# Selective-scan block with sparse attention: states as four n by 32 channels instead of two n by 64, ring buffers cut to four states and two C slots, ScalarE's copies moved one step behind TensorE, tails moved one step earlier

## The reference, cut to what matters

```python
# layer 1, a selective scan (DIN = 256 channels, N = 16 states)
xc, r = split(x @ W_in); xs = causal_conv4(xc) + conv_b; u = silu(xs)
dbc = u @ W_x                       # 128 columns for delta, 16 for B, 16 for C
delta = softplus(dbc[:128] @ W_dt + b_dt)
h[d,n] = exp(delta[d] * A[d,n]) * h[d,n] + delta[d] * u[d] * B[n]     # over 512 tokens
y[d]   = sum_n h[d,n] * C[n] + u[d] * D[d]
x1 = layernorm(x + (y * silu(r)) @ W_out + xs)
# layer 2, on the 64 tokens of each sequence with the highest router score
sel = top_k(x1 @ w_router, 64); attention over the 256 chosen rows, gated MLP, scatter back
out = layernorm(2 * x1 + change)
```

## Time and profile before

| | |
|---|---|
| three runs | 498.07, 494.09, 494.52 us; median 494.52 |
| profiled execution | 495.5 us, of it 493.8 us span from the first to the last instruction |
| mean granted TensorE clock | 0.948 of full |
| busy in the span | TensorE 415.6 us (84%), VectorE 308.5 (62%), ScalarE 310.8 (63%), GpSimd 285.6 (58%) |
| the loop, first to last scan | 58.5 to 345.2 us |
| chain that ended last | TensorE 42%, ScalarE 18%, VectorE 11%, issue 9%, GpSimd 8% |

### The profile page before, as it was taken

The page is one execution under the profiler, slowest core; times in us unless marked ns, Lnnn a source line. Parts: engine busy times, 40 slices in busy tenths (PEclk is TensorE's granted clock), DMA queues, the critical chain, the costliest instruction groups (busy, mean ns, idle before and its releaser), DMA issues.

```text
span 493.8 us, 6513 instructions
## 1 busy us (share of the span) xinstructions
PE 415.6 (84%) x2021; PEld 251.6 (51%) x2021; DVE 308.5 (62%) x600; ACT 310.8 (63%) x674; POOL 285.6 (58%) x261
## 2 busy tenths in 40 slices
PE   5988898799999799799867789775967888999991
PEld 4433453444445344346324356342754767887881
DVE  0302573587666599882689967999387266554355
ACT  4255688983786994476794486961584597543142
POOL 2010187686987889677889769995472144332012
PEclk9998999979999999899997799989987999999997
DMA  6102501005101004201003215760400000000013
GB/s 231 45 0 84 133 23 43 21 2 156 60 23 42 23 1 98 74 24 40 8 17 72 82 41 168 232 263 0 172 0 3 0 1 1 2 0 1 1 43 128
DMA packets 18710, 29.11 MB, mean 59 GB/s; under 512 B 2698, under 2 KB 10676, under 8 KB 18420
## 3 DMA queue, kind: packets, MB, share of 16 engines
q1 hardware_dynamic: 18676, 28.70, 18.6%
HBM read 22.27 MB, written 2.23 MB: 50 GB/s over the span
## 4 chain that ended last, share of the span: by engine, by line
PE 42%; ACT 18%; DVE 11%; issue 9%; POOL 8%; POOLq 0%; DVEq 0%; ACTq 0%
PE bank L536 7%; PE bank L552 6%; ACT loop_buf L1025 5%; ACT front_a L1035 5%; PE bank L673 4%; POOL state L1561 3%; PE bank L849 3%; PE bank L825 3%; PE bank L617 2%; ACT state L1059 2%; PE bank L639 2%; DVE state L1185 2%; PE bank L857 1%; PE bank L574 1%; ACT state L1060 1%
## 5 line engine op out<-in xcount | busy, mean ns | idle before, releaser
L1185 DVE TENSOR_TENSOR_SCAN state<-front_a,bank 128x512 f32<-128x512 f32 x88 | 102.7, 1205 | 44.6 <-PE bank L536 22.9
L536 PEld LDWEIGHTS bank<-ident,loop_buf 128*128 128x128 f32 x512 | 60.5, 146 | 84.4 <-issue 41.2
L536 PE MATMUL bank<-ident,loop_buf 128*128 128x128 f32 x512 | 85.3, 290 | 18.4 <-ACT loop_buf L1025 17.1
L1035 ACT ACTIVATE front_a<-loop_buf,a_neg 128x512 f32<-128x512 f32 x128 | 84.6, 712 | 8.2 <-DVE copy L1185 5.4
L1025 ACT ACTIVATE loop_buf<-copy,b_rows 128x256 f32<-128x256 f32 x190 | 78.9, 495 | 0.1
L552 PE MATMUL bank<-front_c,conv_raw 128*128 128x512 f32 x128 | 60.8, 608 | 3.3 <-ACT front_c L900 2.0
L1185 DVE TENSOR_TENSOR_SCAN copy<-front_a,bank 128x512 f32<-128x512 f32 x40 | 47.3, 1209 | 24.7 <-PE bank L536 11.5
L1561 POOL TENSOR_TENSOR state<-state,front_a 128x1024 f32<-128x1024 f32 x22 | 53.1, 2417 | 9.5 <-DVE state L1185 9.4
L1561 POOL TENSOR_TENSOR state<-state,c_own 128x1024 f32<-128x1024 f32 x22 | 52.0, 2368 | 9.8 <-DVE state L1185 9.1
L673 PE MATMUL bank<-state,fold 128*64 128x512 f32 x176 | 50.2, 648 | 0.8 <-POOL state L1561 0.8
L1574 POOL TENSOR_TENSOR loop_buf<-copy,b_rows 128x512 f32<-128x512 f32 x31 | 33.6, 1083 | 26.0 <-ACT copy L900 23.2
(11 more groups left out here) (203 smaller groups left out, 759.1 us busy)
## 6 DMA issues: line engine op xcount, KB each, us to landing
front_a<-c_stage SPq DMA_DIRECT2D x32, 128.0 KB, 2.8
c_own<-c_stage SPq DMA_DIRECT2D x32, 128.0 KB, 2.9
loop_buf<-front_b SPq DMA_DIRECT2D x32, 128.0 KB, 2.4
copy<-in_L_attn_x SPq DMA_DIRECT2D x4, 512.0 KB, 3.7
front_b<-in_L_ffn_wo SPq DMA_DIRECT2D x1, 2048.0 KB, 10.0
copy<-in_L_ffn_wq SPq DMA_DIRECT2D x1, 2048.0 KB, 8.2
out<-loop_buf SPq DMA_DIRECT2D x3, 512.0 KB, 3.0
conv_raw<-in_L_attn_conv_w SPq DMA_DIRECT2D x2, 512.0 KB, 3.9
```

The source lines that it names most:

```text
L536: return pe.transpose(dst, src, ident[:])
L1035: act.activation(decay[:, u % NDA, :], delta_wide[:, b % 2, k, :], ACT.Exp, scale=a_neg[:, k, m:m + 1]).then_inc(decay_made, 1)
L1185: dve.tensor_tensor_scan(state[t % NH][:, j, :], decay[:, u % NDA, :], bank[BU_BANK[u % NBU]][:], 0.0, ALU.mult, ALU.add).then_inc(scanned, 1)
```

## The change

The state tile becomes four values of n by 32 channels: a group is four n, four groups per batch, eight units per group. `fold` becomes 128 by 32, and one `add_states(w)` serves two steps with four matmuls into the four partition quarters of the bank, at column positions 0, 32, 64, 96; it runs at odd t. Z of a group has four instructions per chunk; ScalarE does one chunk per step in three of four steps, GpSimd one instruction of 1,024 elements per group at t % 4 == 1, no longer one ahead of its turn at t = 0. `delta_wide` has a slot per 32 channels (eight per batch, ring of 12), widened by 32 DMAs of 32 partitions per batch. `c_wide` has two slots, each filled by four DMAs. The state ring has four buffers. SBUF that this frees and needs is balanced by storing x1 of each batch to DRAM and loading all of it back (2 MB) before the output; ScalarE's `la` waits for the previous batch's gather, choice and store. ScalarE drains in step t what belongs to step t-1, between the two decays. Fronts and tails move by up to three steps; four one-hot instructions become one, two rank additions become one reduction. The reload order of weights changes: w_v, w_o, w_dn are issued together, behind the store of b2's x1 and ahead of the last C slot.

```diff
-    -24: ("xT0", "xT1"), ... -13: ("su", "r0", "r1"), -12: ("dt",), -11: ("bc",),
-    -10: ("rs", "cr", "dl0", "dl1"), -9: ("s1",), -8: ("s2",), -7: ("s3",), -6: ("s4",), -5: ("s5", "s6"),
-    -3: ("du0", "du1"),
+    -25: ("xT0", "xT1"), ... -13: ("su", "r0", "r1"), -12: ("dt", "bc"),
+    -10: ("rs", "cr", "dl0", "dl1", "s1"), -9: ("s2",), -8: ("s3",), -7: ("s4",), -6: ("s5", "s6"),
+    -5: ("du0", "du1"),
...
-    2: ("y0", "y1", "g0", "g1"), 4: ("o0",), 5: ("o1",), 6: ("ls0", "ls1"), 7: ("lp0", "lp1"),
-    8: ("la0", "la1"), 9: ("lx0", "lx1", "ld0", "ld1"), 10: ("sb",), 11: ("k0",), 12: ("k1",), 13: ("k2", "k3"),
-    14: ("pf",), 15: ("ga", "cs"),
+    1: ("y0", "y1", "g0", "g1"), 3: ("o0",), 4: ("o1",), 5: ("ls0", "ls1"), 6: ("lp0", "lp1"),
+    7: ("la0", "la1"), 8: ("lx0", "lx1", "ld0", "ld1"), 9: ("sb", "k0", "k1"), 10: ("k2", "k3"),
+    13: ("pf",), 15: ("ga", "cs"),
...
-        NDA, NBU, NH, NZ, NCW = 4, 4, 6, 2, 4
+        NDA, NBU, NH, NZ, NCW = 4, 4, 4, 2, 2
+        KB, NDW = 4 * KD, 12
...
+            def widen_delta(b, h):
+                sp.wait_ge(delta_ready, KD * b + h + 1)
+                for j in range(4):
+                    slot = KB * b + 4 * h + j
+                    if slot >= NDW:
+                        b0, k0 = (slot - NDW) // KB, (slot - NDW) % KB
+                        sp.wait_ge(decay_made, 2 * NST * b0 + KB * (NQ - 1) + k0 + 1)
+                    for i in range(4):
+                        sp.dma_start(delta_wide[slot % NDW][i * QP:(i + 1) * QP, :],
+                                     delta[j * QP:(j + 1) * QP, h, :]).then_inc(in_delta[4 * h + j], 16)
+            def store_x1(b):
+                sp.wait_ge(rows_ready, 2 * (b + 1))
+                sp.dma_start(x1_stage[b], x1[:, :, 0:DM]).then_inc(x1_stored, 16)
...
+            widen_delta(0, 0)
+            widen_delta(0, 1)
             load_x(2)
+            for g in range(NCW, B * NQ - 2):
+                b, m = g // NQ, g % NQ
                 widen_c(g)
+                if m == 0:
+                    widen_delta(b, 1)
+                elif m == 2 and b >= 1:
+                    store_x1(b - 1)
+                elif m == 3:
+                    if b == 0:
+                        load_x(3)
+                    widen_delta(b + 1, 0)
+            widen_c(B * NQ - 2)
+            store_x1(B - 2)
...
             load("w_v", w_v, wv.rearrange("(k p) n -> p k n", p=P))
-            widen_c(B * NPAIR - 3)
             load("w_o", w_o, wo.rearrange("(h p) n -> p h n", p=P))
-            widen_c(B * NPAIR - 2)
             load("w_dn", w_dn, w_down.rearrange("(f p) n -> p f n", p=P))
-            widen_c(B * NPAIR - 1)
+            widen_c(B * NQ - 1)
...
+            store_x1(B - 1)
+            sp.wait_ge(x1_stored, 16 * B)
+            sp.dma_start(x1_all, x1_stage.rearrange("b p c d -> p b c d")).then_inc(x1_loaded, 16)
...
-                for j in range(2):
-                    mm = pe.matmul(bank[Y_BANK[h]][j * P // 2:(j + 1) * P // 2, :], fold[:], state[t % NH][:, j, :],
-                                   start=(m == 0), stop=(m == NPAIR - 1))
+                pe.wait_ge(weighed, 2 * w + 2)
+                for j in range(4):
+                    mm = pe.matmul(bank[Y_BANK[h]][j * QP:(j + 1) * QP, :], fold[:],
+                                   state[:, (2 * w + j // 2) % NH, j % 2, :], start=(m == 0), stop=(m == NQ - 1),
+                                   tile_position=(0, j * QP))
...
-                if t >= LAG_ADD:
-                    add_states(t - LAG_ADD)
+                if t % 2 and t >= 3:
+                    add_states((t - 3) // 2)
...
+                    if b >= 1:
+                        wait_filled(act, ("ga", b - 1))
+                        act.wait_ge(chosen_ready, b)
+                        act.wait_ge(x1_stored, 16 * b)
...
-                for u in range(2 * t + 2, min(2 * t + 4, NU)):
-                    make_decay(u)
-                if t % 2 == 0 and t < T_LAST - 1:
-                    for c in range(C - 1):
-                        make_z(t // 2 + 1, c)
-                for b, piece in tails(t):
-                    tail(b, piece)
...
+                if 2 * t + 2 < NU:
+                    make_decay(2 * t + 2)
+                drain(t - 1)            # ScalarE's tails, fronts and h1T copy of step t - 1
+                if 2 * t + 3 < NU:
+                    make_decay(2 * t + 3)
+                if t // 4 + 1 < B * NQ and t % 4 < C - 1:
+                    make_z(t // 4 + 1, t % 4)
...
                 if t >= NH and j == 0:
-                    dve.wait_ge(summed, t - NH + 1)
+                    dve.wait_ge(summed, (t - NH) // 2 + 1)
...
-                    link(dve.tensor_tensor(ranks[:, 0, :], ranks[:, 0, :], ranks[:, 1, :], ALU.add))
-                    link(dve.tensor_tensor(ranks[:, 2, :], ranks[:, 0, :], ranks[:, 2, :], ALU.add))
-                    dve.tensor_scalar(chosen[:], ranks[:, 2, :], float(K), None, ALU.is_lt).then_inc(chosen_ready, 1)
+                    link(dve.tensor_reduce(rank_sum[:], ranks[:].rearrange("p a c -> p c a"), AX.X, ALU.add))
+                    dve.tensor_scalar(chosen[:], rank_sum[:], float(K), None, ALU.is_lt).then_inc(chosen_ready, 1)
...
-                    link(dve.memset(ranks[:, 0, 0:1], 0.0))
...
-                    for c in range(C):
-                        dve.tensor_scalar(onehot[:, b // 2, c, r:r + K], slot_no[:], place[:, c:c + 1], None,
-                                          ALU.is_equal).then_inc(onehot_ready, 1)
+                    dve.tensor_tensor(onehot[:, b // 2, :, r:r + K], slot_no[:].unsqueeze(1).to_broadcast(shape),
+                                      place[:].unsqueeze(2).to_broadcast(shape), ALU.is_equal).then_inc(onehot_ready, 1)
...
-                if t == 0:
-                    make_z(1)
-                elif t % 2 and t // 2 + 2 < B * NPAIR:
-                    make_z(t // 2 + 2)
+                if t % 4 == 1 and t // 4 + 1 < B * NQ:
+                    make_z(t // 4 + 1)
```

180 lines of the change are left out of this document (90 added, 90 removed), and 4 rows, old and new, of the table FRONT_AT.

## The result

The changed kernel takes 502.44 us (median, 501.02 to 504.46) against 495.24 for the kernel before in the same session: ratio 1.017, 95% interval 1.0134 to 1.0205. The forecast was 475.5 and faster. It is slower, by 7 to 8 us, and outside the range.

What follows compares the result with a forecast made beforehand. No single bound: TensorE, VectorE and GpSimd take turns, the busiest engine filling 93% of the loop. Terms -10 - 8 - 9 + 0 + 3 + 3 + 2 = -19 from 494.5 gave 475.5 us, range 461 to 489, with rival cases 460 to 494.

Steps and rivals of the forecast that it cites:

- Step 1: TensorE's sum over n: eight matmuls at four column positions serve two steps in about 1.01 us; -10 us, ends 0 and -32.
- rival of pairs: Sum over n: column tiles still go in pairs, so its saving is 0; 485.5 us, chance 0.10.
- Step 2: ScalarE: Z in even portions and copies one step late halve TensorE's 16.6 us wait for Z; -8 us, ends 0 and -16.6.
- step 6: State ring: with four buffers for six, scans wait when GpSimd trails; +3 us, ends 0 and +26.
- step 3: VectorE's small work in the tails: fewer rank and one-hot instructions save 3 us in each of three; -9, ends -3 and -17.
- Step 4: GpSimd's Z: two instructions become one of 1,024 elements; 0 us, at worst +3.
- Step 5: Entry: first batch's delta in 32 transfers, eighth decay not before 73.1 us; +3 us, up to +6.
- rival of the ring: State ring in n8 to n15 of b0 to b2: scans wait for a sum behind late products; slower, 508.5 us, chance 0.14.
- Step 7: Exit: weight loads issued later, behind x1's store, with the last C slot queued behind them; +2 us, ends 0 and +8.
- a second way: Whole loop: subtract savings from each half batch's busiest engine, keep 93%; loop 262 us, 24 shorter, with entry and exit -19.

Runs made afterwards that it cites:

- b_halffold: Kernel before, with the sum over n made on half the columns in the six middle pairs of each batch: 491.55 us, 0.9963.
- b_slfold: Kernel before, with VectorE's small work cut, ScalarE's copies one step late and the sum over n on half the columns in six middle pairs: 473.76 us, 0.963.
- b_smalllag: Kernel before, with VectorE's small work cut and ScalarE's copies made one step late, in the old order of the state: 477.92 us, 0.967.
- a_nolag: Changed kernel, with ScalarE doing tails and fronts in the same step as TensorE, still between the two decays: 527.2 us, 1.0693.
- a_entry: Changed kernel, with half of the first batch's 32 delta copies issued by GpSimd's queue instead of SyncE's: 498.94 us, 1.011.

## Why the prediction was wrong, step by step

Two readings were off before any step. GpSimd has 33 us of busy time in three of the eight half batches and not in four; the fourth has 30.6. And the scans' wait for the sum was 3.8 us, of which the row of 1.9 is half. Neither changes the sum.

**Step 1 (sum over n, -10).** The mechanism was right: four matmuls start within 0.02 us of each other, the next four 0.45 us later, and the eight take 1.06 us (1.01 for four before), so the rival of pairs is out. No gap shows at the switch back (the last sum matmul ended at 104.58, the next transpose had begun at 104.52). The value was too high: 24 us less of these matmuls gave 2.8 and 4.2 us by the medians of b_halffold and b_slfold, so for 32 us some -4 to -6. I took half of the chain's share of L673. The chain counts what ran last; it does not say that the next engine would have been ready. And a part was taken back with the clock: the sums' own busy time fell by 30.0 us (72.7 to 42.7), but TensorE's in the loop by 18.6 only. The mean sum matmul rose from 648 ns to 745, the mean convolution matmul from 608 to 632.

**Step 2 (Z in even portions and copies one step late, -8).** This is the step that failed, together with a term that is missing (under step 6). The lag itself gained (-3.7, -2.0 behind step 3). But of the tables I wrote that TensorE's needs had been given "one or two steps more in the tables, so no new wait is seen there". I checked TensorE's needs of ScalarE and not GpSimd's. GpSimd's s2 and s3 wait for ScalarE's exponential and logarithm, which the lag makes a step later while the table draws s1 into dl's step; GpSimd then stood 14.0 us for the exponential and 5.7 for the logarithm where it had stood 6.1 and 4.5, with products and the tail behind it. The front's table cost about 4 us in the changed kernel, the tail's perhaps 3.5 (not clear of the uncertainty). The 5.6 us for the ranks and the 14.6 for the front's table are losses in the old order and no terms of this one. The lag alone does not make GpSimd wait (6.4 and 4.5 us in b_smalllag), nor does the table alone (0.9 and 6.2 in a_nolag); lag and table together do. TensorE's wait for ScalarE's Z came down from 16.6 to 8.9 in the loop, as forecast, and three waits for GpSimd's Z, 8.3 us, took their place.

**Step 3 (small work, -9).** Right in kind, within its ends, and too small: -14.4, measured alone. The one-hot instruction takes 0.42 to 2.13 us, the ranks chain 4.3, under the 6 named. I priced the instructions that go and not the ones behind them, which then come before GpSimd's next product.

**Step 4 (GpSimd's Z, 0).** Right: 15 of 1.96 us for 31 of 1.083, 4 us less of GpSimd's work.

**Step 5 (entry, +3).** Right in mechanism: the eighth decay began at 72.62 (73.1 was worked out). 6 us were lost in n0 to n3, at the upper end of what I named (+6), and 3.5 came back in a_entry.

**Step 6 (four buffers, +3) and the rival of the ring.** The rival forecast 508.5 with over 22 us of scans waiting for the sum; 36.5 us were seen and 502.4 measured. So the sign that I had named for this rival came, but its price did not hold for the ring alone: a fifth buffer took every one of these waits away and no time. What I had not priced is that the merged sum runs one step nearer to the second product. Moving it, with the fifth buffer in place, gave 8.6 us. I gave the order of the sum no term at all, and this is the largest loss that a run gave back.

**Step 7 (exit, +2).** It cost nothing that shows: b3 took 62.9 for 62.4, and from the loop's end on the kernel is 3.6 us shorter. w_v was issued at 329.29 and the last C slots landed by 347, and GpSimd waited 0.2 us for them.

In sum: steps 2 (the lag), 3 and a small step 1 are worth some -20 by the single runs; the merged sum's place (+7 to 9), the tables (+4, perhaps 7.5), the entry (+3.5), and a rest of some 7 to 13 that is open bring it to +7 to 8. The repairs do not add, so this is a rough account and no proof. The chances stood on engine sums ("93% of the busiest engine"), a second way that shared the first one's error: it takes for granted that waits shrink along with work.

## What to carry to other kernels

Where several engines take turns, as here, price an edit by the order of each engine's list: for every piece that moves or comes late, ask what stands behind it on that engine, and who waits for that. When two pieces of a change touch the same chain (a lag here, a table there), count the steps between producer and consumer for all pairs of engines, not for the bottleneck alone. And run the small, safe part of a change by itself: here it was worth 14.4 us for the 9 forecast and was buried under the rest. Last, the engine that a wait is put down to is only the one that came last: take that wait away in a run before you believe it. Here 36.5 us of waits went and no time with them.

## What the runs showed that I had not expected

TensorE's granted clock went with its work and its waits. With 24 us less work and all else equal the granted clock of the loop fell from 0.97 to 0.92; with 15.5 us more it rose from 0.86 to 0.90; after 5.77 us of idling four transposes took 1.06 us and not 0.60. Of the work saved on TensorE, which waits here for others, most was given back. Second, a copy's issue on SyncE takes 0.63 us for 64 KB as for 128 KB (20.26 us for 32, 4.99 for 8), so the first batch's delta, in four times as many transfers of half the size, took four times the issuing time.
